# Routed experts of a two-layer decoder: 39 tiles with a weight set each, in place of 23 pairs of tiles

## What is computed

```python
router_logits = x_flat @ gate_w.T                      # 2048 rows, 8 experts
top_w, sel = jax.lax.top_k(router_logits, 2)
top_w = jax.nn.softmax(top_w, axis=-1)
tw = jnp.zeros((n, 8)).at[tok_ids, sel].add(top_w)
g = jnp.einsum('nd,efd->enf', x_flat, gate_proj)       # d = 512, f = 352
u = jnp.einsum('nd,efd->enf', x_flat, up_proj)
h = jax.nn.silu(g) * u
eo = jnp.einsum('enf,edf->end', h, down_proj)
out = jnp.einsum('end,ne->nd', eo, tw)
```

## Time and profile before

| | us |
|---|---|
| median of the three runs | 3479.44 |
| lowest and highest | 3477.32, 3481.93 |
| the profiled execution, its own time | 3482.6 |
| span of its profile | 3480.8 |
| expert stage, first gate product to last result copy | 3080 to 3413 |

### The profile page before, as it was taken

One profiled execution on the slowest core, in us unless ns is written; L12 is line 12 of the kernel. 1 busy time (PEld: TensorE's weight loads), 2 busy tenths in 40 slices (PEclk: granted clock), 3 DMA queues, 4 the chain that ended last, 5 costly groups with the idle time before them and its releaser, 6 DMA issues. The chain is left out here.

```text
span 3480.8 us, 58860 instructions
## 1 busy us (share of the span) xinstructions
PE 3159.6 (91%) x21152; PEld 2638.6 (76%) x21152; DVE 2094.4 (60%) x3767; ACT 1278.2 (37%) x3276; POOL 1450.4 (42%) x1470
## 2 busy tenths in 40 slices
PE   7999999999969999799896999699999999869991
PEld 6887878878847777678685777488888888758881
DVE  5666566576645776421064777556667678645656
ACT  3333333333346666201102333244444444324430
POOL 4454343344422434300153222355555556544445
PEclk9999999999989999789998999799999999979996
DMA  4001016022310111339563112211101001156665
GB/s 172 18 16 51 0 35 232 0 95 102 141 33 24 53 32 57 144 100 340 171 143 115 37 42 63 99 56 34 36 12 47 12 24 43 39 199 223 225 221 157
DMA packets 137872, 317.18 MB, mean 91 GB/s; under 512 B 18425, under 2 KB 30457, under 8 KB 135538
## 3 DMA queue, kind: packets, MB, share of 16 engines
q1 hardware_dynamic: 120194, 274.61, 23.4%
q0 software_dynamic: 15360, 36.25, 3.9%
q10 hardware_dynamic: 2160, 4.21, 0.4%
HBM read 231.07 MB, written 98.04 MB: 95 GB/s over the span
## 5 line engine op out<-in xcount | busy, mean ns | idle before, releaser
L398 POOL TENSOR_TENSOR a_sq<-a_tq,a_sinq 128x256 f32<-128x256 f32 x128 | 150.3, 1194 | 358.4 <-DVE a_tq L474 358.4
L398 POOL TENSOR_TENSOR a_sk<-a_tk,a_sink 128x256 f32<-128x256 f32 x128 | 123.8, 986 | 90.0 <-DVE a_tk L474 90.0
L364 ACT COPY a_probT<-bank 128x512 f32<-128x512 f32 x64 | 37.6, 587 | 328.3 <-PE bank L713 328.3
L411 POOL TENSOR_TENSOR e_sk<-e_tk 128x512 f32<-128x512 f32 x64 | 66.6, 1040 | 204.6 <-DVE e_tk L501 204.6
L353 ACT ACTIVATE e_prob<-bank,e_nb,e_rq 128x128 f32<-128x128 f32 x256 | 113.9, 455 | 86.7 <-DVE e_nb L575 86.7
L348 ACT ACTIVATE a_sm<-a_sm,a_nmax 128x128 f32<-128x128 f32 x256 | 99.8, 391 | 121.7 <-DVE a_nmax L570 121.7
L952 ACT ACTIVATE b_prob<-bank,b_nb 128x128 f32<-128x128 f32 x512 | 139.4, 387 | 11.6 <-DVE b_nb L1148 11.3
L1046 POOL TENSOR_TENSOR d_prob<-d_prob,d_nmax 128x1024 f32<-128x1024 f32 x32 | 64.0, 1999 | 183.3 <-DVE d_nmax L1143 183.3
L2340 POOL TENSOR_TENSOR n_wu_lo<-nw_wu,n_wu_hi 128x1408 fp32r<-128x1408 f32 x23 | 74.0, 3218 | 135.4 <-DVE n_wu_hi L2384 135.4
L496 DVE TENSOR_TENSOR a_kr<-a_kr,a_sk 128x512 f32<-128x512 f32 x64 | 66.4, 1037 | 89.0 <-POOL a_sk L398 89.0
L1145 DVE TENSOR_REDUCE b_nmax<-bank 128x8 f32<-128x1024 f32 x64 | 77.9, 1217 | 68.6 <-PE bank L1289 67.9
(11 more groups left out here) (512 smaller groups left out, 10718.8 us busy)
## 6 DMA issues: line engine op xcount, KB each, us to landing
packed<-all_zero SPq DMA_DIRECT2D x32, 1024.0 KB, 8.3
cw_wg<-in_c_wg SPq DMA_DIRECT2D x32, 512.0 KB
cw_wu<-in_c_wu SPq DMA_DIRECT2D x32, 512.0 KB
cw_wd<-in_c_wd SPq DMA_DIRECT2D x32, 512.0 KB
nw_wg<-in_f_wg SPq DMA_DIRECT2D x23, 704.0 KB
nw_wu<-in_f_wu SPq DMA_DIRECT2D x23, 704.0 KB
nw_wd<-in_f_wd SPq DMA_DIRECT2D x23, 512.0 KB
nw_xe<-packed SPq DMA_DIRECT2D x46, 256.0 KB, 2.7
```

The lines of the kernel that those rows point to most:

```text
L364: nc.scalar.copy(probT[:], pP[:, :]).then_inc(act_pt, 1)
L398: step = nc.gpsimd.tensor_tensor(o, i, s, ALU.mult)
```

## The change

Tiles of 128 rows take the place of pairs of 256. `NT2` = 39 tiles are enough for any routing. Each tile has its own set of weights, loaded and split for it alone.

- `end_of_routing` makes its tables for 39 tiles: 16 limits for each expert (`PER`) in place of 8, tables of 39 x 8 in place of 23 x 8. Its SP program loads the weights of tiles 0 and 1 and x tiles 0 to 3, one x tile after each set and then two more.
- In `routed_experts` the weight buffer of tile t is t % 2. SP's `refill(i, n)` for tile t loads the x tile t+4 after x of t is transposed, then waits for all four splits of t (v_gate, g_u, g_d and a new v_d) and loads the weights of tile t+2. SP runs refill(t+2) ahead of store(t).
- ACT splits gate and down weights of t+1 in every slot t, with `take_y` of t-1, moved here from DVE, between the two.
- DVE's slot t begins with `split_up` of t+1, then the low part of x, of h, `split_gate` of t+1, h of t, and ends with a new `split_d` of t: the 96x512 piece of the low part of the down weights, moved here from POOL.
- POOL makes the low part of the up weights and of the 128x1024 piece of the down weights for each tile.
- PE waits for the splits in every slot, in place of every second one.

```diff
@@ end_of_routing
-            for w in range(2):
-                weights.load(sp, weights.number(sp, 0, w), w)
-                if w == 0:
+            for n in range(4):
+                if n < 2:
+                    weights.load(sp, weights.number(sp, n), n)
+                if n == 0:
                     sp.wait_ge(router.sent, 16 * K * B)
-                weights.load_x(sp, router.packed.rearrange("(t r) d -> t r d", r=P), weights.place(sp, 0, w), w)
+                weights.load_x(sp, router.packed.rearrange("(t r) d -> t r d", r=P), weights.place(sp, n), n)
...
@@ routed_experts, sync
-            def refill(i, w):
-                e, t = weights.number(sp, i + 1, w), weights.place(sp, i + 1, w)
-                sp.wait_ge(pe_x, done(R * i + 2 * w + 1))
-                weights.load_x(sp, packed, t, w)
-                sp.wait_ge(v_gate, done(2 * i + w))
-                sp.wait_ge(g_u, done(2 * i + w))
-                sp.wait_ge(g_d, done(2 * i + w))
-                weights.load(sp, e, w)
-                for n in (2 * w, 2 * w + 1):
+            def refill(i, n, weighted=True, x=True):
+                t = R * i + n
+                if weighted:
+                    number = weights.number(sp, t + 2)
+                if x:
+                    place = weights.place(sp, t + 4)
+                    sp.wait_ge(pe_x, done(t))
+                    weights.load_x(sp, packed, place, n % R)
+                if weighted:
+                    for split in (v_gate, g_u, g_d, v_d):
+                        sp.wait_ge(split, done(t))
+                    weights.load(sp, number, n % 2)
+            for n in range(2):
+                refill(0, n)
+            ahead = (NT - 6) // R
+            with sp.Fori(0, ahead) as i:
+                for n in range(R):
+                    refill(i, n + 2)
                     store(i, n)
...
@@ routed_experts, scalar
+            def take_y(i, n):
+                act.wait_ge(pe_o, done(R * i + n))
+                act.wait_ge(y_out[n], landed(i))
+                nc.scalar.copy(ye[:, n, :], pO[n % 2][:, :]).then_inc(act_y, 1)
...
-                next_pair = (i, 1) if n < 2 else (i + 1, 0)
-                if not (isinstance(i, int) and later(i, n) > LAST):
-                    (split_gate if n % 2 == 0 else split_d)(*next_pair)
+                if ahead:
+                    split_gate(*following(i, n, R))
+                if back:
+                    take_y(*preceding(i, n, R))
+                if ahead:
+                    split_d(*following(i, n, R))
...
@@ routed_experts, vector
+            def split_d(i, n):
+                dve.wait_ge(act_d, done(R * i + n))
+                o, x, y = (each_down(t["d"], n % 2)[1] for t in (lo, raw, hi))
+                nc.vector.tensor_tensor(o, x, y.bitcast(F32), ALU.subtract).then_inc(v_d, 1)
...
             def slot(i, n, back=True, ahead=True):
                 t = R * i + n
                 if ahead:
+                    split_up(*following(i, n, R))
                     take_x(*following(i, n, R))
-                if n % 2 and not (isinstance(i, int) and later(i, n) > LAST):
-                    split_gate(*((i, 1) if n == 1 else (i + 1, 0)))
                 if back:
                     take_h(*preceding(i, n, R))
+                if ahead:
+                    split_gate(*following(i, n, R))
                 dve.wait_ge(act_g, done(t))
                 dve.wait_ge(pe_u, done(t))
                 nc.vector.tensor_tensor(h[:, n % 2], gate[:, n % 2], pU[n % 2][:, 0:F], ALU.mult).then_inc(v_h, 1)
-                if n % 2 == 0 and not (isinstance(i, int) and later(i, n) > LAST):
-                    split_up(*((i, 1) if n == 0 else (i + 1, 0)))
-                if back:
-                    take_y(*preceding(i, n, R))
+                split_d(i, n)
...
@@ routed_experts, tensor
                 pe.wait_ge(v_hl, done(t))
-                if n % 2 == 0:
-                    pe.wait_ge(g_d, done(2 * i + n // 2))
-                pe.wait_ge(v_y, done(t - 2))
+                pe.wait_ge(g_d, done(t))
+                pe.wait_ge(v_d, done(t))
+                pe.wait_ge(act_y, done(t - 2))
...
-NP2 = (2 * B * P + 8 * (2 * P - 1)) // (2 * P)
+NT2 = (2 * B * P + 8 * (P - 1)) // P
```

More of the change, by code:

```diff
@@ L2002, in _ @@
             router.place(dve, LAST)
-            step(vec.tensor_tensor(full[:], carry[:, B].unsqueeze(2).to_broadcast(each), limit[:], ALU.is_gt))
-            step(vec.tensor_reduce(npair[:], full[:], AX.X, ALU.add))
-            step(vec.tensor_tensor(summed[:], upto[:], npair[:].unsqueeze(1).to_broadcast(each), ALU.mult))
+            step(vec.tensor_tensor(full[:], carry[:, B].unsqueeze(2).to_broadcast(tiles), limit[:], ALU.is_gt))
+            step(vec.tensor_reduce(ntile[:], full[:], AX.X, ALU.add))
@@ L2015, in _ @@
-            step(vec.scalar_tensor_tensor(out=tsum[:], in0=texp[:], scalar=float(REGION // PAIR), in1=tsum[:], op0=ALU.mult, op1=ALU.add))
-            vec.tensor_scalar(weights.tile[:], tsum[:], 2.0, float(NE * REGION // P - 2), ALU.mult, ALU.min).then_inc(tabled, 1)
-            step(vec.scalar_tensor_tensor(out=npair[:], in0=first[:, 0:NE], scalar=float(PAIR), in1=region[:], op0=ALU.mult, op1=ALU.subtract))
-            step(vec.tensor_tensor(prod[:], hot[:], npair[:].unsqueeze(1).unsqueeze(1).to_broadcast([P, K, B, NE]), ALU.mult))
+            step(vec.tensor_tensor(tsum[:], iota[:, 0:NT], tsum[:], ALU.subtract))
@@ new lines, in _ @@
+            step(vec.scalar_tensor_tensor(out=tsum[:], in0=texp[:], scalar=float(PER), in1=tsum[:], op0=ALU.mult, op1=ALU.add))
+            vec.tensor_scalar(weights.tile[:], tsum[:], float(NE * PER - 1), None, ALU.min).then_inc(tabled, 1)
+            step(vec.scalar_tensor_tensor(out=ntile[:], in0=first[:, 0:NE], scalar=float(P), in1=region[:], op0=ALU.mult, op1=ALU.subtract))
+            step(vec.tensor_tensor(prod[:], hot[:], ntile[:].unsqueeze(1).unsqueeze(1).to_broadcast([P, K, B, NE]), ALU.mult))
@@ L2248, in routed_experts @@
         gate_in, up_in, d_in, each_down = weights.gate_in, weights.up_in, weights.d_in, weights.each_down
[L2249 to L2251 removed]
+        act_gate, act_d, v_gate, v_up, v_d, g_u, g_d = st.sems("act_gate", "act_d", "v_gate", "v_up", "v_d", "g_u", "g_d")
+        pe_x, pe_g, pe_u, pe_h, pe_o, act_x, act_g, act_h, act_y, v_x, v_h, v_hl = st.sems(
+            "pe_x", "pe_g", "pe_u", "pe_h", "pe_o", "act_x", "act_g", "act_h", "act_y", "v_x", "v_h", "v_hl")
         block = ctx.enter_context(nc.Block())
[L2254 to L2255 removed]
         @block.sync
@@ L2332, in _ @@
             take_h(*LAST)
+            take_y(*LAST)
         @block.gpsimd
@@ L2711, in decoder @@
             weight, rows = sc.sbuf("weight", [P, B, 2]), sc.sbuf("rows", [P, B, 2], U32)
-            expert, tile = (sc.sbuf(n, [P, NP2], I32) for n in ("expert", "tile"))
+            expert, tile = (sc.sbuf(n, [P, NT2], I32) for n in ("expert", "tile"))
             with ExitStack() as routed:
                 weights = RoutedWeights(Stage(nc, routed, "nw"), w, expert, tile)
-                end_of_routing(nc, "r", psum, router, weight, rows, weights, NP2)
-                routed_experts(nc, psum, ident, packed2.rearrange("(t r) d -> t r d", r=P), result2, weights, NP2)
+                end_of_routing(nc, "r", psum, router, weight, rows, weights, NT2)
+                routed_experts(nc, psum, ident, packed2.rearrange("(t r) d -> t r d", r=P), result2, weights, NT2)
             combine(nc, "fc", xall, result2, rows, weight, out, 2)
```

139 lines of the change are left out of this document (60 added, 79 removed).

## The result

The changed kernel takes 3657.33 us (median of four runs, 3655.80 to 3658.17), the kernel before on the same chip 3480.68 us: a ratio of 1.0502, interval 1.0487 to 1.0518. It is 5% slower. The forecast was 3728 us, 71 us too much, in a range from 3635 to 3800. The profiled execution took 3655.8 us with a span of 3654.0.

What follows compares the result with a forecast made beforehand. TensorE was taken to bound the kernel before; afterwards a closed loop of 0.4 + 8.0 + 6.7 = 15.1 us a tile, 37 times from 3091, ends the stage 248 us later: 3728 us, range 3635 to 3800.

Steps and rivals of the forecast that it cites:

- The bound before and what it takes out: Expert stage bound by TensorE at 6.99 us a tile; seven of 46 tiles fewer take out 49 us of its work.
- The loop: SP, DMA, DVE, SP closes once per tile: load issued after split_d, needed by the next split_up; 15.1 us a tile.
- the case that I called the forecast: The closed loop sets a period of 13.0 to 16.9 us, total 3650 to 3795 us; chance 0.74.
- Step 1: SP, from v_d to the issue of the gate weights: 0.4 us.
- Step 2: From the issue of the gate weights to the landing of the up weights: 8.0 us, bounds 6.0 and 9.1.
- Steps 3 and 4: DVE from landing to slot end: 6.1 us with split_gate held by POOL's subtraction, then split_d 0.6, reaching 6.7.
- Who else could be late: No other engine sets the period: TensorE at most 14.0 us a tile at a lower clock, ScalarE and POOL hidden.
- T(0): Moment at which DVE ends slot 0 of the expert stage: about 3091 us (3089 to 3093).
- T(37): Moment at which DVE ends slot 37, the last paced by the loop: 3650 us, with the stage's end at 3660.
- The race for the port: POOL's split_d starts before DVE's and holds DVE for 2.48 us: period 17.6, total 3820 us; chance 0.09.
- The shorter loop: Transfer runs as in the first load and POOL hardly meets DVE: period about 12 us, total 3613; chance 0.10.
- The faster case: SP releases the load early enough to hide it, DMA engines set the pace: total 3452 us; chance 0.05.

Runs made afterwards that it cites:

- e1: Changed kernel with gate and up weights loaded once their own splits are done, only down weights waiting for g_d and v_d: ratio 1.0074 to the kernel before.
- e9: Changed kernel with half of each tile's gate and up weights not loaded from tile 2 on: ratio 1.0300 to the kernel before.
- e5: Changed kernel with the x tile (0.26 MB) loaded right ahead of the weights instead of before the waits for the splits: ratio 1.0603 to the kernel before.
- e4: Changed kernel with POOL's subtraction for the up weights cut from 1408 to 16 columns: ratio 1.0283 to the kernel before.
- e8: Changed kernel with 40 identity transposes added on TensorE ahead of each tile's down products: ratio 1.0550 to the kernel before.
- e12: e10 with the cast of the up weights on ScalarE and POOL's subtraction of the up weights on DVE: ratio 0.9896 to the kernel before.
- e2: e1 with SP issuing gate and up weights of tile t+2 first, then down weights of t+1: ratio 1.0059 to the kernel before.
- e10: e1 with SP reading tables ahead and issuing down (t+2), gate and up (t+3), x (t+5), store (t-1): ratio 1.0051 to the kernel before.
- e11: e10 with the cast of the up weights on ScalarE in place of DVE: ratio 0.9938 to the kernel before.
- e6: The kernel before with the two x loads of a pair moved behind its weight load: ratio 0.9987 to the unedited kernel before.

## Why the prediction was right, and where its size was off

**The bound before and what it takes out.** Not refuted; TensorE at 6.99 us a tile was the pace. Seven tiles less of it are not to be seen, because the pace was lost.

**The loop.** Right, and the core of the matter. The cast waits in 37 of 39 cases, as named. e1 undoes this and gives back 4.3 of 5%. The mechanism was no luck; that the time still fell into the case that I called the forecast was, in part. That case began at 3650 us and a period of 13.0, and 0.2 us less of transfer in each period would have left it.

**Step 1**, SP: 0.4 forecast, 0.23 measured. 37 x 0.17 = 6 us.

**Step 2**, from the issue to the landing: 8.0 forecast, 6.20 measured in the period shown and 6.3 in the mean of the loads. This is the term that was mis-sized: 37 x 1.7 = 63 us of the 71 by which the median was missed. The two bounds stood in the sum, 6.0 from the first load and 9.1 from the loop, and I chose the one nearer in place, on the ground that the loop has compute beside the transfer. The right one was the one nearer in the state of the queue: in the changed kernel nothing is under way when the load is issued, as at the first load. One microsecond each after the issue at 3310.57 in the changed kernel:

```profile
3310.00:3311.00 1.00, 1.00 (x7) 1.00 (x6) 0.34 (x1) 0.86 (x2) 0.00 (x0) 0.50 0.00 0
3311.00:3312.00 1.00, 1.00 (x7) 1.00 (x7) 0.00 (x0) 1.00 (x2) 0.00 (x0) 0.87 0.36 73
3312.00:3313.00 1.00, 1.00 (x9) 0.98 (x8) 0.00 (x0) 0.68 (x2) 0.73 (x1) 1.00 0.86 315
3313.00:3314.00 1.00, 1.00 (x9) 1.00 (x8) 0.00 (x0) 0.89 (x3) 1.00 (x1) 1.00 1.03 428
```

The queue is empty at the issue (0 GB/s), and 3 us later it moves 428 GB/s, with POOL and ScalarE at work. In the earlier trace rows 0.52 MB of x stood ahead of the weights. From 3165 to the landing 2.77 MB passed there; in the changed kernel it was 1.72 MB from the issue to the landing:

```profile
3310.57:3316.77 6.20, 4.72 (x29) 4.42 (x27) 0.00 (x0) 4.36 (x8) 2.40 (x1) 0.94 0.80 277
```

The two landings are 2.9 us apart, and the 1.05 MB more are worth 3.1 us at the 340 GB/s of e9 (an estimate, as two more things differ: in the earlier trace rows data flowed in the first microsecond after the issue already, and then at 300 GB/s on average). So most of the difference goes with the bytes that passed before the up weights had landed. x ahead is only a part of them: e5's 0.26 MB cost 0.35 us, so 0.52 MB would be 0.7. The other half MB are down weights and results, which were issued behind. Why more of them had passed there than here, and why weights behind x run at 318 GB/s and not at 373, stays open.

The page "DMA: Bandwidth & Descriptors" of the Trainium skill (Anatomy of one DMA) gave an estimate of 5.3 us by its fixed part and rate, which it has for transfers issued by GpSimd, while SyncE issues these. The estimate was nearer than my choice, but 0.9 below the 6.20 measured, and the row of the first load (6.0) was nearer still.

**Steps 3 and 4**, DVE: 6.7 forecast, 6.67 measured, and each piece as worked out: gate split 3.69 against 3.7, which ends 1.48 after POOL's end (3309.30 against 3307.82), the same distance as in the earlier trace rows; n_wd_lo 0.68 against 0.6. e4 shows the share of POOL by itself.

The full lock of the page "SBUF — State Buffer" of the Trainium skill (Who interferes with whom) agrees with these rows but for the 0.15 us at the end. What I did not draw from it before is that the locked times of two engines make one budget, as in the table above.

**Who else could be late.** TensorE's clock fell, to 0.79, and cost nothing: e8. TensorE was busy for 70%, not under 55%, since I had put it at full clock in a longer period: 6.99 us of work took 9.2. The DMA engines moved 205 GB/s, not 180, as the period was shorter.

**The sum.** Own time forecast 3731, measured 3655.8, 75 less: 70 from the period (15.1 against 13.2, 37 times), 4 from T(0), which was 3087.3 for 3091; the first gate product too was 4.8 us earlier than in the earlier trace rows's kernel, 3075.30 against 3080.08, so this is no effect of the stage. From T(37) to the end of the last copy it took 10.3 us for 10.

**The rivals.** The race for the port, POOL's down piece ahead of DVE's, was not seen. DVE's n_wd_lo took over 3 us, its sign, only once, in the first tile, and there it was POOL's up piece that held it; the down piece came after:

```profile
3082.18 4.58 POOL L2352 TENSOR_TENSOR n_wu_lo<-nw_wu,n_wu_hi 128x1408 fp32r<-128x1408 f32 x1
...
3084.05 3.26 DVE L2395 TENSOR_TENSOR n_wd_lo<-nw_wd,n_wd_hi 96x512 fp32r<-96x512 f32 x1
...
3086.72 2.84 POOL L2357 TENSOR_TENSOR n_wd_lo<-nw_wd,n_wd_hi 128x1024 fp32r<-128x1024 f32 x1
```

In the loop DVE was always first (0.68). POOL's piece starts 8.4 us after the cast of the up weights (median), where I had 6.5, and DVE's 6.0. e8 shows that this is the slower TensorE: at a clock of 0.99 POOL's piece starts at 6.6, and DVE's again at 6.0. So the margin that I gave, 0.4, was about right for a fast TensorE, and the point against the race, that a slower one adds almost 2 us, was right too. The shorter loop had the transfer right and POOL's part wrong; the truth lay between it and the forecast. By my own sign, 6.4 us of wait a cast for the shorter loop and 8.4 for the forecast, the measured 6.5 points to that rival's transfer. The faster case needed the load to be hidden and a bound by the transfers; e12 is that case, made by hand, and 3441.6 us is a little better than the 3452 worked out for it, which goes with transfers at 365 GB/s and not the 341 of the earlier trace rows.

## What to carry to other kernels

When a load is released by the last instruction of an engine's slot and used by the first of its next, the whole time from issue to landing is in every period, however idle the engines look; count that loop first, and release each buffer by its own last reader. Take the duration of a transfer from a row in which the queue has the same things ahead of it, not from the row that is nearest in place, and compare the bytes that passed up to the landing. And where VectorE and GpSimd both work from SBUF to SBUF (here float32 casts and subtractions), add their times up as if they were one engine before giving either more work; ScalarE stands outside of that sum.

## What the runs showed of the hardware

- VectorE and GpSimd together: periods of 8.77 to 8.92 us for a sum of 8.80 (e1, e2, e10) and 7.83 for 7.91 (e11). An engine that is shut out shows as busy (a cast of 0.89 us as 2.47), so DVE's 89% in e10 was no sign of its own work.
- Loads into an idle queue reached 428 GB/s three microseconds after the issue, and a stage full of them kept up 365 GB/s (e12), where the other expert stage had 341. With 0.52 MB of x issued 1.2 us ahead, loads ran at 318 GB/s from 2 to 8 us behind their issue, with x behind them at 373 (e6).
- A granted clock of 0.79 in place of 0.99 changed the time of the stage from first to last cast by 0.3 us of 494: a clock is only worth what TensorE is on the path.
